# Gather stages of a two-image attention and deformable-convolution kernel: unrolled code rewritten as short loops, corner sums of the 64-channel stage moved to TensorE

## The reference

```
samp[c, k, pix] = sum over 4 corners q of  w[pix, k, q] * h[c, corner_q(y, x)]     (64 channels: also * mask[pix, k])
out[o, pix]     = sum over c, k of          samp[c, k, pix] * weight[o, c, k]
```

## Time and profile before

| what | us |
|---|---|
| median of three runs | 6745.91 |
| the profiled execution, whole | 6749.49 |
| its span, first to last instruction | 6747.7 |
| 64-channel gather stage, first image, first gather to last `residual` | 1784.1 to 2254.4 |
| 256-channel gather stages, first image, first gather to last DVE sum | 2422.4 to 2807.4 and 2980.4 to 3371.6 |
| mean granted TensorE clock over the span | 0.889 of full |

### The profile page before, as it was taken

One profiled execution on the slowest core, in us unless ns is written; L12 is line 12 of the kernel. 1 busy time (PEld: TensorE's weight loads), 2 busy tenths in 40 slices (PEclk: granted clock), 3 DMA queues, 4 the chain that ended last, 5 costly groups with the idle time before them and its releaser, 6 DMA issues. The chain is left out here.

```text
span 6747.7 us, 126038 instructions
## 1 busy us (share of the span) xinstructions
PE 5426.3 (80%) x38156; PEld 3715.8 (55%) x38156; DVE 4983.7 (74%) x12163; ACT 3474.2 (51%) x6593; POOL 2026.8 (30%) x2338
## 2 busy tenths in 40 slices
PE   5999989998533679878869999899984336798798
PEld 3777757776322444454437777577753225444544
DVE  4999979996333479759959998799953334797698
ACT  3888868885100135425538887688841001354254
POOL 0000000000377247427600000000003772573275
PEclk9999999999655789989989999999996557899899
DMA  2000000000222379759910000000002224797699
GB/s 66 3 3 3 3 21 3 4 3 28 63 82 82 115 277 409 288 194 410 379 48 3 3 3 3 21 3 4 3 27 67 82 82 121 288 409 271 212 410 361
DMA packets 369615, 819.33 MB, mean 121 GB/s; under 512 B 109347, under 2 KB 196710, under 8 KB 368387
## 3 DMA queue, kind: packets, MB, share of 16 engines
q0 software_dynamic: 193536, 679.59, 26.4%
q1 hardware_dynamic: 175874, 137.17, 7.3%
HBM read 709.75 MB, written 94.26 MB: 119 GB/s over the span
## 5 line engine op out<-in xcount | busy, mean ns | idle before, releaser
L1476 DVE TENSOR_SCALAR_CACHE_REDUCE arena<-ps 128x512 f32<-128x512 f32 x2048 | 1395.5, 682 | 89.4 <-DVEq L1475 87.3
L1496 DVE TENSOR_TENSOR arena<-ps,arena 128x512 f16<-128x512 f32 x2048 | 1405.3, 687 | 32.4 <-DVEq L1495 21.9
L637 POOL DMA_INDIRECT arena<-corners,arena x1152 | 1092.9, 949 | 984.7 <-POOLq L628 597.4
L767 PEld LDWEIGHTS ps<-arena 128*128 128x128 f16 x16384 | 1057.0, 98 | 553.3 <-issue 242.0
L1031 ACT ACTIVATE arena<-arena 128x1024 f32<-128x1024 f32 x1024 | 1175.6, 1148 | 324.0 <-ACTq L1029 324.0
L1038 ACT ACTIVATE arena<-ps 128x512 f16<-128x512 f32 x2048 | 1187.6, 592 | 234.8 <-ACTq L1037 219.9
L752 PE MATMUL ps<-arena 128*128 128x512 f16 x4096 | 1224.3, 381 | 85.1 <-PEq L750 81.8
L767 PE MATMUL ps<-arena 128*128 x16384 | 1248.9, 219 | 14.2 <-PEq L763 12.8
L781 PE MATMUL ps<-ident_s,arena 128*128 128x128 f32 x8192 | 1244.4, 274 | 0.3 <-issue 0.3
L1165 ACT ACTIVATE ps<-arena 128x256 f32<-128x256 f32 x1152 | 549.0, 478 | 1015.7 <-DMA arena<-corners,arena 985.0
L946 PE MATMUL ps<-arena 128*128 128x512 f32 x2304 | 1054.3, 601 | 0.0
(11 more groups left out here) (131 smaller groups left out, 4291.6 us busy)
## 6 DMA issues: line engine op xcount, KB each, us to landing
corners<-arena SPq DMA_DIRECT2D x256, 256.0 KB, 3.9
arena<-corners,arena POOLq DMA_INDIRECT x1728, 8.8
arena<-arena SPq DMA_DIRECT2D x192, 64.0 KB, 1.9
arena<-in_wd SPq DMA_DIRECT2D x4, 2304.0 KB, 8.2
X<-in_x SPq DMA_DIRECT2D x2, 4096.0 KB, 12.4
attn_scratch<-arena SPq DMA_DIRECT2D x256, 32.0 KB, 1.5
arena<-attn_scratch SPq DMA_DIRECT2D x16, 512.0 KB
corners<-arena SPq DMA_DIRECT2D x128, 64.0 KB, 2.2
```

What stands on the lines that cost most here:

```text
L637: pool.indirect_dma_start(G3[slot].rearrange("p a c -> p (a c)"), None, table256, bass.IndirectOffsetOnAxis(ap=IDX3[:, 4 * g + t, k:k + 1] ...
L767: last = mm(ps[:, 6 + p, 0:2 * D], part[:, g % 4, k * 128:(k + 1) * 128], V[:, bass.ds(j * NHEAD + 2 * pair + h, 1), :, :].rearrange("p o ...
L1476: v.tensor_scalar(S[p][:, g * CHUNK:(g + 1) * CHUNK], ps[:, g % 2, :], float(D) ** -0.5 / QK_SCALE ** 2, -3.0e38, ALU.mult, ALU.max, accum ...
L1496: v.tensor_tensor(P2[:, g % 4, :], ps[:, 2 + g % 4, :], P1[:, g % 4, :], ALU.subtract).then_inc(p2_ready, 1)
```

## The change

All gather stages become loops on every engine, and every counter that grew through a stage becomes a semaphore that is counted down where it is waited for. Where two or three engines wait for one event, SP takes the event and passes it on.

64-channel stage:
- ACT copies the indices (`IS2`, four slots, filled four tiles ahead), POOL only waits for `is_ready`. The memsets of `SM2` go, one for five index rows comes.
- The weights are copied to PSUM (`ps[:, 5, ...]`), and the multiply reads them there. Its output goes to `PR2`, split by corner. The two adds go.
- PE sums the corners: `summed` does, for each of five pieces, four accumulating matmuls of `PR2` by the identity, which also transposes. It works one tile ahead of `mixed`, into two PSUM bank pairs; a last `summed` behind tile 31 works on old data and is not used.
- SP turns `weighted` into `pr_ready` (PE) and `g2_free` (POOL).

256-channel stage:
- Loops of three steps, nested in a loop over chunks on ACT and DVE; nine steps to an iteration on PE. The ring has 12 buffers (three steps), `SAMP` and `ST` have three.
- Indices (`IS3`) and weights (`WS3`) of a step are copied by ACT, two small instructions a step; `corners` writes `IDX3` and `W4_3` in the order of use.
- ACT waits for both gathers of a half before its two products.
- SP turns `half_done` (a half's sums done) into `acc_free` (ACT), `samp_ready` (PE) and `g_free` (POOL, two buffers), and `evicted` into `o_free`.
- The output accumulators are PSUM banks 6 and 7 alone, so that a chunk's first tap waits for the eviction of the chunk before.

```diff
-        NG = 16
+        NG = 12
...
 # SP, 64 channels
+                with sp.Fori(0, NT) as t:
+                    sp.wait_ge(weighted, 1)
+                    sp.sem_inc(weighted, -1)
+                    sp.sem_inc(pr_ready, 1)
+                    sp.sem_inc(g2_free, 1)
+                sp.sem_inc(pr_ready, 1)
...
 # SP, 256 channels
+                    def samples_done():
+                        sp.wait_ge(half_done, 1)
+                        sp.sem_inc(half_done, -1)
+                        sp.sem_inc(acc_free, 1)
+                        sp.sem_inc(samp_ready, 1)
+                        sp.sem_inc(g_free, 2)
+                    def group_done(g):
+                        for oh in range(CH):
+                            sp.wait_ge(evicted, 1)
+                            sp.sem_inc(evicted, -1)
+                            sp.sem_inc(o_free, 1)
+                            if layer == 1:
...
+                    with sp.Fori(1, NCH) as g:
+                        with sp.Fori(0, 4) as i:
+                            samples_done()
+                        group_done(g - 1)
+                        with sp.Fori(4, 2 * KK) as i:
+                            samples_done()
...
 # POOL, 64 channels
-                with pool.Fori(0, NT // 2) as t2:
-                    for p in range(2):
+                with pool.Fori(0, NT // 4) as t4:
+                    for q in range(4):
+                        p = q % 2
+                        pool.wait_ge(is_ready, 1)
+                        pool.sem_inc(is_ready, -1)
                         pool.wait_ge(g2_free, 1)
                         pool.sem_inc(g2_free, -1)
-                        pool.tensor_copy(IS2[p], IDX2[:, bass.ds(2 * t2 + p, 1), :]
-                                                                 .rearrange("p a k -> p (a k)")).then_inc(pool_step, 1)
-                        pool.wait_ge(pool_step, 1)
-                        pool.sem_inc(pool_step, -1)
                         for k in range(KK):
                             pool.indirect_dma_start(G2[p][:, k, :], None, table64,
...
 # POOL, 256 channels
+                    with pool.Fori(0, TAPS // 3) as i:
+                        for k in range(3):
+                            pool.wait_ge(is_ready, 1)
+                            pool.sem_inc(is_ready, -1)
                             for t in range(4):
-                                if j >= 4:
-                                    pool.wait_ge(samp_ready, 4 * (j - 4) + t + 1)
+                                if t % 2 == 0:
+                                    pool.wait_ge(g_free, 2)
+                                    pool.sem_inc(g_free, -2)
                                 pool.indirect_dma_start(
...
 # PE, 64 channels
+                def summed(p):
+                    pe.wait_ge(pr_ready, 1)
+                    pe.sem_inc(pr_ready, -1)
+                    for i in range(5):
+                        rows = 128 if i < 4 else CB
+                        for q in range(4):
+                            last = mm(ps[0:rows, 6 * p + i // 4, (i % 4) * 128:(i % 4 + 1) * 128],
+                                      PR2[p][:, q, i * 128:i * 128 + rows], ident_s[:, :],
+                                      start=(q == 0), stop=(q == 3))
+                    last.then_inc(smt_ps, 1)
...
+                summed(0)
                 with pe.Fori(0, NT // 2) as t2:
                     for p in range(2):
+                        summed(1 - p)
+                        mixed(p)
...
 # PE, 256 channels
+                    with pe.Fori(0, NCH) as g:
+                        for k in range(KK):
+                            pe.wait_ge(st_ready, CH)
+                            pe.sem_inc(st_ready, -CH)
+                            transposes((k + 1) % 3)
+                            tap(k)
...
 # ACT, 64 channels
+                def staged2(t, q):
+                    p = q % 2
+                    act.wait_ge(smt_ps, 1)
+                    act.sem_inc(smt_ps, -1)
+                    act.sem_inc(pr_free, 1)
+                    af(SMT2[p][:, 0:4, :].rearrange("p a b -> p (a b)"), ps[:, 6 * p, :],
+                       ACT.Copy).then_inc(smt_ready, 1)
+                    af(SMT2[p][0:CB, 4, :], ps[0:CB, 6 * p + 1, 0:128], ACT.Copy).then_inc(smt_ready, 1)
+                    af(IS2[:, q, :], IDX2[:, bass.ds(t + 4, 1), :].rearrange("p a k -> p (a k)"), ACT.Copy).then_inc(is_ready, 1)
...
 # ACT, 256 channels
+                    def products(i, k):
+                        act.wait_ge(act_step, 1)
+                        act.sem_inc(act_step, -1)
+                        for h in range(2):
+                            act.wait_ge(acc_free, 1)
+                            act.sem_inc(acc_free, -1)
+                            act.wait_ge(g_ready[k][h], (i + 1 + (2 * b + layer) * (TAPS // 3)) * 32)
+                            act.sem_inc(gathers_seen, 1)
+                            for t in (2 * h, 2 * h + 1):
+                                af(ps[:, h, (t % 2) * C:(t % 2 + 1) * C], G3[4 * k + t][:, 0, :], ACT.Copy,
+                                       scale=WS3[:, k, 4 * t:4 * t + 1]).then_inc(prod_ready, 1)
+                        weights(3 * i + k + 1, (k + 1) % 3)
+                        af(IS3[:, k, :], IDX3[:, bass.ds((3 * i + k + 3) * 4, 4)], ACT.Copy).then_inc(is_ready, 1)
...
 # DVE, 64 channels
+                def weigh(t, turn, p):
+                    w = ps[:, 5, p * KK * 4:(p + 1) * KK * 4]
...
+                    v.tensor_tensor(PR2[p].rearrange("p q (k c) -> p k q c", k=KK),
+                                    G2[p].rearrange("p k (q c) -> p k q c", q=4),
+                                    w.rearrange("p (k q) -> p k q", q=4).unsqueeze(3).to_broadcast([128, KK, 4, CB]),
+                                    ALU.mult).then_inc(weighted, 1)
...
 # DVE, 256 channels
+                    def three(evict=None):
+                        for k in range(3):
+                            sampled(k, 0)
+                            if k == 1 and evict is not None and layer == 1:
+                                output(evict)
+                            sampled(k, 1)
+                    with dve.Fori(0, 3) as k3:
+                        three()
+                    with dve.Fori(1, NCH) as g:
+                        three(evict=g - 1)
+                        with dve.Fori(1, 3) as k3:
+                            three()
```

More of the change, by code:

```diff
@@ new lines, in mixed @@
+                def mixed(p):
+                    pe.wait_ge(smt_ready, 2)
+                    pe.sem_inc(smt_ready, -2)
+                    for i in range(5):
+                        rows = 128 if i < 4 else CB
+                        last = mm(ps[0:CB, 2, 0:128], w2_s[0:rows, i, :], SMT2[p][0:rows, i, :],
+                                  start=(i == 0), stop=(i == 4))
+                    last.then_inc(d_ready, 1)
+                    pe.wait_ge(h2_ready, 1)
+                    pe.sem_inc(h2_ready, -1)
+                    pe.wait_ge(e_free, 1)
+                    pe.sem_inc(e_free, -1)
+                    for oh in range(CH):
+                        last = mm(ps[:, 3 + p, oh * 128:(oh + 1) * 128], w3_s[:, oh * 128:(oh + 1) * 128],
+                                  H2[p], start=True, stop=True)
+                    last.then_inc(e_ready, 1)
@@ L890, in _ @@
-                        for oh in range(CH):
-                            last = mm(ps[:, 3 + p, oh * 128:(oh + 1) * 128], w3_s[:, oh * 128:(oh + 1) * 128],
-                                      H2[p], start=True, stop=True)
-                        last.then_inc(e_ready, 1)
+                        summed(1 - p)
+                        mixed(p)
+                pe.wait_ge(smt_ready, 2)
+                pe.sem_inc(smt_ready, -2)
                 pe.drain().then_inc(arrived, 1)
@@ L948, in tap @@
                                           start=(k == 0 and half == 0), stop=(k == KK - 1 and half == CH - 1))
[L949 to L951 removed]
+                            if k == KK - 1:
+                                last.then_inc(o_ready, 1)
+                        if k < KK - 1:
+                            last.then_inc(st_free, 1)
                     transposes(0)
[L954 to L958 removed]
@@ L1177, in output @@
                     def output(g):
                         for oh in range(CH):
[L1180 to L1192 removed]
+                            act.wait_ge(o_ready, 1)
@@ new lines, in output, with three @@
+                            act.sem_inc(o_ready, -1)
+                            if oh == CH - 1:
+                                act.sem_inc(st_free, 1)
+                            af(OUT[:, oh, chunk(g)], ps[:, 6 + oh, :], ACT.Identity,
+                                    bias=vec_s[:, B1, oh:oh + 1]).then_inc(evicted, 1)
+                    def three(i, begins=False, evict=None):
+                        for k in range(3):
+                            products(i, k)
```

(14 more changed lines are left out.)

272 lines of the change are left out of this document (117 added, 155 removed).

## The result

The changed kernel takes 6559.7 us (median of 4 runs, 6550.4 to 6562.6), the kernel before 6745.4 beside it (4 runs): ratio 0.9722, 95% interval 0.9705 to 0.9739. Forecast were 6547 us and a range of 6515 to 6640. The profiled execution took 6562.6 us, 186.9 less than the 6749.5 of before.

What follows compares the result with a forecast made beforehand. POOL was taken to bound the 64-channel stage, the DMA engines the 256-channel stage. 6749.5 - 174.6 - 32.8 + 8 = 6550.1 us on the profiled execution, 3.6 above the median, so 6547 us; range 6515 to 6640.

Steps and rivals of the forecast that it cites:

- The tile, 11.27 us: 64-channel stage: POOL's tile falls from 14.3 us to nine gathers at 1.25 us, 360 us for the stage against 455.
- 2.04 + 0.25 + 0.73: 64-channel tile, us removed: gather stalls behind the multiply (2.04) and line 1566 (0.25), POOL's index copy and idle time (0.73).
- PE and its clock: 64-channel stage: clock rises within each tile; PE needs 10.7 us even at half clock for half its work, under POOL's 11.27.
- rival B: 64-channel stage: PE stays at half clock and bounds it, 13.3 us a tile, 6692 us in all; 7 in 100.
- The end of the stage, 23 us: 64-channel stage: last gather's end to last residual takes 23 us, between 21.7 (full clock) and 33 (half), against 15.2.
- -174.6: 64-channel stage: 470.3 us becomes 360 + 23 = 383, -87.3 an image, -174.6 for both.
- 256-channel, -32.8: 256-channel stage: loops fetch no instructions, so the sums' excess of 9.1 and 7.3 us goes, -16.4 an image, -32.8 for both.
- 9 x 1: 256-channel first layer: 26 instruction packets, 9 of 16 KB and 17 of 8 KB; 9 x 1 us is the excess.
- The ends, +8: Four stages, +2 us each: +1.5 at the stage's ends and +0.5 in `corners` for scattered writes.
- Rival C: 64-channel stage: new multiply holds up POOL as the old did, 13.3 us a tile, 6679 us; 6 in 100.
- D: 256-channel stage: longer chain of DVE, SP, ACT sets a pace over the DMA's; 6656 us at 5.5 a step; 9 in 100.
- E: Slower than before: jumps in the short loops fetch code, 6867 us if 80 back edges a stage all fetch; 4 in 100.

Runs made afterwards that it cites:

- e1: Changed kernel with the 36 weights of a tile copied to SBUF instead of PSUM: 6653.9 us, ratio to before 0.9867.
- e2: Kernel before with only the 36 weights of a tile moved from SBUF to PSUM: 6667.0 us, ratio to before 0.9886.
- the ladder: 64-channel tile times by run: 14.31 us before; 13.05 weights in PSUM; 12.04 additions gone to TensorE; 11.27 index copies gone to ScalarE.
- e6: Changed kernel with POOL's wait for the last index copies of the 64-channel stage moved behind the barrier: 6545.5 us, ratio to before 0.9706.
- e5: Changed kernel with the 256-channel loops of TensorE, ScalarE, VectorE and POOL all written out: 6581.4 us, ratio to before 0.9756.
- e4: Changed kernel with only TensorE's loop over the chunks of a 256-channel layer written out: 6557.6 us, ratio to before 0.9721.

## Why the prediction was right, point by point

- **The tile, 11.27 us**: measured 11.27. The stall behind line 1562 went for the reason given, the PSUM operand, which was an inference from line 1654 and is now shown from both sides (e1, e2). As prices for each edit alone the terms 2.04 + 0.25 + 0.73 don't hold, only their sum: in the order of the ladder the weights bring 1.26, the additions 1.01, the copies 0.77, and taken away last (e1) the weights bring 1.5. Read from one timeline, a stall shows what it costs beside the others, not what it costs alone.
- **PE and its clock**: rival B fell. A tile takes 6.5 us of sums on average and 3.0 of mixing, 0.9 of that a wait for ScalarE: 9.4 of 11.27 us, 1.9 of room, where the forecast had 10.7. At full clock throughout it would be 4.83 and 3.0, close to the forecast's 8. The forecast that each rise puts PE back under POOL's pace is what the tiles show; it had left open whether a tile starts at half clock, and 7 in 10 do.
- **The end of the stage, 23 us**: 23.3 and 22.6. To hit it within 0.4 was in part luck: `summed(31)` took 7.37 and 6.72 for 6.5, the unused one 4.7 for 5.5, and runs of the same code have tails from 20.7 to 23.5, by the clock at the last tile. First gather to last residual 383.9 and 383.2 against 470.2 before, -173.3 for both images; forecast -174.6.
- **Missed: POOL's drain**. The working counted POOL's waits inside the loop and not the wait behind it, in front of a drain of 5.9 us that had been hidden. +3.5 us a stage, +7 (e6).
- **256-channel, -32.8**: measured 1524.1 - 1498.3 = 25.8. The cause, fetches, was an inference and is borne out by e5. "9 x 1" of the 26 packets, which the forecast did not tell apart, is also what the landings show: nine jumps of about 1 us, at packets of 8 KB. That it was TensorE's nine of 16 KB, as the expectation of e4 has it, was wrong; they cost 1.1 us together. What the sum had too large is that all of the excess goes: over the undisturbed 367.3 and 376.3 the changed layers still lie 0.9 to 2.1 us, about 6 in all, after four to seven packets each, and the second image had 1 less to lose than the first. Steps of some 6 us at a chunk's end stay as well, but steps of 4.7 behind them make them good.
- **The ends, +8**: PE ends 1.3 us later behind VectorE in four layers, +5.3. `corners` is 0.4 longer in two of its six places and as before in the others, +0.8, so that the 0.5 a stage of the forecast was mostly not there.
- Together: -173.3 + 7 - 25.8 + 5.3, and 3.3 us more ahead of the first 64-channel stage, which other runs of the same code there don't have (its barrier is passed at 1766.7 in e6, 1775.1 changed): -183.5 of the -186.9. The forecast on the same execution was -199.4; the 12.5 between are the drain 7, the fetches 7, that 3.3 and 1.3 of the 64-channel stage, less 2.7 by which the ends cost less (`corners` not counted) and 3.4 that stay unplaced.
- **Rival C** (new multiply holds up POOL) is what e1 makes of the kernel, 6653.9; priced at 6679. **D** fell: ACT waits for landings at DMA share 1.00. **E** fell: 4 packets in the layer's window. The rule of the Trainium skill, "Runtime: NRT & Kernel Launch", section Instruction fetch mechanics, that prefers unrolling to jumps, holds the other way here: with all loops written out the sums are 25.4 us longer.

## What to carry to other kernels

While POOL makes DMA descriptors, keep one of the two inputs of the long VectorE instructions beside it in PSUM, and look at all of them: when one stall goes, the next instruction with both inputs in SBUF takes it up. In a stage bound by its DMA engines loops were worth more here than written-out code, by 25 us over four layers. Look at the landings engine by engine: a gather is complete when the slowest of 16 is. Before crediting an edit with a shorter tail, see whether TensorE's clock was the same in both runs. When a wait is added at the end of a stage, look at what stands behind it on that engine; and measure on more than one chip before a gain is promised, since here 2.8% on one was nothing on another.

## What the runs showed of the hardware that was not expected

- POOL's drain behind indirect DMAs lasts 5.94 us even 21 us behind the last gather (6.59 in the 256-channel stage), at most 0.83 in stages without them.
- A gather that starts within a VectorE instruction with two inputs in SBUF ends 0.81 to 0.83 us behind that instruction's end, whatever its length (2.56 or 1.36 us), in all 248 cases of the kernel before, e1 and e2; one already under way is 0.03 us longer at most. The weights' copy, SBUF to SBUF with one input and 0.4 us long, holds up none of the 16 that start within it.
- Instruction packets of 8 KB, 0.3 us each, put one DMA engine behind the other 15 by about 1 us at a time, 9 us by the end of a layer, and each gather waits for it. Nine of 16 KB, 1.1 us each, cost 1.1 us in all.
- On one of the chips TensorE all but stands still while POOL makes descriptors (one matmul in 0.7 us or more, signals up to 17 us late), with no wait and no packet shown; the stages without gathers that were compared are as fast as elsewhere (from the first 64-channel stage's barrier to the first 256-channel gather 167 us on both).
